# A fused attention and expert kernel on one Trainium2 core: the norms' work divided anew between VectorE and GpSimd, the finish of a batch at other steps, scatters at other places

## The chip, the cores and the metric

The kernel runs on 1 core of one Trainium2 chip. Its time is device microseconds of one launch, and of each version the median of several runs is given. Engines are TensorE (PE), VectorE (DVE), ScalarE (ACT), GpSimd (POOL) and SyncE (SP). Each runs its own instruction list in order, and semaphores tie the lists together.

## The reference

Input is `x`, 8 batches of 512 rows by 256 numbers, f16.

```
x = x + layernorm(attention(layernorm(x)))      # 16 heads of 16, causal, biases, f16
x = x + layernorm(ffn(layernorm(x)))            # 8 experts, 256 -> 688 -> 256, float32

layernorm(x) = (x - mean) / sqrt(var + 1e-5)    # along the 256
ffn: logits = x @ Ws + bs; the two best experts of each row, their logits through a softmax;
     out = sum over the two of weight * ((silu(x @ Wg[e]) * (x @ Wu[e])) @ Wd[e])
```

There are three norms per batch before the expert part's output: of the input (attention's own input), of the attention's output, and of the sum of the two (the experts' input). A fourth, of the experts' output, is done at the end in another way and isn't touched.

## The kernel before

**Groups and steps.** The attention part is 8 batches b of 4 groups g (four heads each), and a group is 12 steps. At each step TensorE computes one bank of transposed scores of this group (L1774), one bank of plain scores of the group two ahead (L1777), and from step 8 on products with the values (L1784). ScalarE turns each bank of transposed scores into exponentials in `pT` (L983). VectorE takes the row maxima of the plain scores (L1149, and L1162 from group 18 on), which TensorE needs two steps later. GpSimd sets to zero what lies above the diagonal: three cuts (L759) per group, released by steps 3, 7 and 11 of the exponentials. TensorE's values at step 8 wait for cut 0, those at step 10 for cut 1, those at step 2 of the next group for cut 2. A place in the lists below is a pair (group of the batch, step) or, for GpSimd, (group, cut).

**Everything else is woven in by hand-written lists** of such pairs: `EARLY_AT` and `TILE_AT` (TensorE's projections and transposes, before and from group 18 on), `AT_NEXT_NORM` (the input norm of batch b+1), `AT_FINISH` (12 parts that finish batch b-1: bias of the attention's output, statistics in two halves, moments, scaling in two halves, adding x, then again statistics, moments, and scaling into `rows`, the experts' input `xn2`), `AT_PLAN` (from batch 3 on, four parts that plan which expert the next tiles belong to), `AT_ROUTE` and `AT_SLOTS` (the choice of experts and of the row's place, in group 3), and `AT_SCATTER` (GpSimd's indirect DMAs of the routed rows to DRAM, 8 per batch in 4 pairs, from batch 2 on).

**From group 18 on** the first expert tiles (256 rows each) run beside the attention: TensorE's products (L1724, L1742), ScalarE's tanh and copies (L943, L955), VectorE's gate and product (L1338, L1346), and on GpSimd after each cut a subtraction (`tile_low`, L775), after cut 0 the scatter of the tile before (`store_tile`, two indirect DMAs, L785), and after cut 1 the taking over of the next tile's row numbers (`take_tile`, L768, L769). SyncE loads a tile once its plan is there and enough scatters have landed (L556 to L566). After group 31 the remaining tiles run alone to about 840 us, and then comes the last norm.

**A norm** is made in four stages. VectorE: statistics (`norm_stats`, L1115) and moments `mv` (`norm_moments`, L1122). GpSimd: `rsqrt` (L692 to L700), which adds epsilon to the variance, copies the mean, takes the power 0.5 and then the power -1. VectorE: `norm_scale` (L1125 to L1132), with mean and `rstd` as scalars per row. TensorE: transposes. `rsqrt` stands at three places in GpSimd's list: for the input norm ahead of cut (0, 0); for the norm of the attention's output after cut (1, 1) and the tile's work there; for the experts' input norm after cut (2, 0) and the tile's work there, so ahead of cut (2, 1). TensorE transposes the experts' input at step 11 of group 2 (`xn2T`), and ScalarE copies it out.

`hold` (L74) is a wait on a semaphore and one increment behind it, used where an instruction reads what its own engine has just written.

## Time and profile before

| | |
|---|---|
| median of 3 runs | 889.12 us (882.86 to 891.24) |
| profiled execution | 878.99 us, of which 877.2 us are its span |
| TensorE's clock granted, mean | 0.917 of full |
| TensorE, VectorE, ScalarE, GpSimd busy | 713.8, 615.1, 550.6, 444.1 us |
| woven part (attention and first 14 tiles) | to about 594 us |
| tiles alone, last norm | about 594 to 840 us, 840 to 877 us |

Times in rows are microseconds from the start of the span unless marked ns. "Idle before <- releaser" is how long an engine had stood before an instruction and whose signal came last. The clock granted is given in parts of 2.4 GHz: 1.00 is 2.4, 0.50 is 1.2 GHz. To separate the groups, the stretches of the tables run from ScalarE's eviction of the shifted queries in one group (L896, once per group, at step 7 or 8) to that in the next: 119.66, 131.08 and 148.83 us are those of groups 1, 2 and 3 of batch 1; 354.05, 373.41, 396.47 and 419.14 those of batch 5.

### The profile page before, as it was taken

The numbers are of one execution on the slowest core, as the hardware profiler recorded it, in microseconds if no ns is written. First come the engines' busy times: TensorE is split into PE (matmuls) and PEld (weight loads), VectorE is DVE, ScalarE is ACT, GpSimd is POOL, SyncE is SP. The second block draws the span as 40 slices with busy tenths as digits, with TensorE's granted clock in tenths as the row PEclk, the third lists the DMA queues.
The fourth block names the chain that finished last, engine by engine and source line by source line (L and its number), as shares of the span: only waits on it lengthen the run. The fifth ranks groups of instructions, "written<-read, shape, count | busy, mean of one in ns | idle before, by whom it ended". The sixth has DMA issues, their size and how long they took to land.

```text
span 877.2 us, 21718 instructions
## 1 busy us (share of the span) xinstructions
PE 713.8 (81%) x6822; PEld 470.2 (54%) x6822; DVE 615.1 (70%) x1960; ACT 550.6 (63%) x1122; POOL 444.1 (51%) x552
## 2 busy tenths in 40 slices
PE   3677677768777989988997899898979999999920
PEld 1244444444443355544554455466857888888810
DVE  5777898888877878897889778755744445444445
ACT  4588885857765667756676576565545555555536
POOL 3554433553624435664577457747564343343427
PEclk9689998998986599999999899999999999999965
DMA  6434231463251111221122021213345233232257
GB/s 194 139 118 147 91 115 44 147 191 108 94 174 49 35 31 21 44 55 20 20 43 52 11 32 38 53 23 56 50 99 145 44 43 45 44 46 42 38 138 268
DMA packets 74008, 69.09 MB, mean 79 GB/s; under 512 B 6832, under 2 KB 67888, under 8 KB 73904
## 3 DMA queue, kind: packets, MB, share of 16 engines
q1 hardware_dynamic: 60624, 53.23, 19.7%
q0 software_dynamic: 13280, 14.49, 11.6%
q8 instruction: 63, 1.03, 0.5%
q14 instruction: 41, 0.34, 0.1%
HBM read 34.04 MB, written 31.29 MB: 74 GB/s over the span
## 4 chain that ended last, share of the span: by engine, by line
PE 46%; DVE 31%; issue 8%; ACT 7%; POOL 5%; DMA 2%; SPq 0%; DVEq 0%; POOLq 0%; ACTq 0%
PE bank L1880 13%; PE bank L1902 10%; PE bank L1724 6%; DVE nmax L1149 5%; DVE unused L1162 5%; PE bank L1631 4%; PE bank L1742 3%; DVE stats L1115 3%; DVE stage L1338 2%; POOL gu_part L862 2%; DVE rows L1130 2%; PE bank L1662 2%; DVE gu_part L1364 2%; PE bank L1591 2%; PE bank L1618 1%
## 5 line engine op out<-in xcount | busy, mean ns | idle before, releaser
L983 ACT ACTIVATE pT<-bank 128x512 f16<-128x512 f32 (+1 forms) x384 | 200.0, 534 | 97.3 <-PE bank L1631 95.0
L759 POOL TENSOR_SCALAR_AFFINE_SELECT pT<-pT 128x512 f16<-128x512 f16 x128 | 87.9, 731 | 146.2 <-ACT pT L983 145.9
L1149 DVE TENSOR_REDUCE nmax<-bank 128x1 f16<-128x384 f32 (+2 forms) x216 | 126.2, 597 | 35.6 <-PE bank L1620 33.6
L1880 PE MATMUL bank<-tile_xT,gu_part 128*128 128x256 f16 (+1 forms) x1100 | 132.4, 275 | 6.9 <-DVE stage L1450 3.6
L1880 PEld LDWEIGHTS bank<-tile_xT,gu_part 128*128 (+1 forms) x1100 | 106.5, 100 | 29.9 <-issue 8.4
L1162 DVE CUSTOM_DVE_ANT_0 unused<-bank,mask 128x384 f16<-128x384 f32 (+2 forms) x224 | 103.5, 483 | 16.5 <-PE bank L1609 15.1
L1450 DVE SCALAR_TENSOR_TENSOR stage<-bank,stage 128x512 f32<-128x512 f32 (+1 forms) x100 | 55.5, 555 | 80.4 <-ACT stage L1036 70.4
L785 POOL DMA_INDIRECT expert_rows<-tile_y,tile_dest x52 | 83.4, 1603 | 55.0 <-ACT tile_y L968 46.4
L1902 PE MATMUL bank<-wd_part,stage 128*128 (+2 forms) x850 | 105.3, 277 | 2.5 <-ACT stage L1045 1.7
L1724 PE MATMUL bank<-tile_xT,gu_part 128*128 128x256 f16 (+1 forms) x616 | 90.2, 286 | 12.8 <-DVE stage L1346 12.3
L1902 PEld LDWEIGHTS bank<-wd_part,stage 128*128 128x128 f16 (+2 forms) x850 | 78.2, 99 | 23.4 <-issue 13.8
L1045 ACT ACTIVATE stage<-stage 128x512 f16<-128x512 f32 (+1 forms) x100 | 52.3, 523 | 57.8 <-DVE stage L1450 53.2
L1457 DVE TENSOR_TENSOR stage<-stage 128x512 f16<-128x512 f32 (+1 forms) x100 | 55.8, 558 | 37.3 <-ACT stage L1045 34.4
L1662 PEld LDWEIGHTS bank<-va,pT 128*128 128x128 f16 x1280 | 54.5, 98 | 46.9 <-issue 26.9
L1662 PE MATMUL bank<-va,pT 128*128 128x17 f16 x1280 | 67.5, 173 | 12.7 <-POOL pT L759 12.7
L145 POOL DMA_INDIRECT dispatch_rows<-rows,slot x64 | 66.8, 1043 | 19.7 <-issue 16.8
L1724 PEld LDWEIGHTS bank<-tile_xT,gu_part 128*128 (+1 forms) x616 | 58.1, 103 | 29.8 <-issue 18.7
L1631 PE MATMUL bank<-qT,kT 32*128 32x512 f16 (+3 forms) x256 | 72.7, 325 | 0.6 <-issue 0.3
L1742 PE MATMUL bank<-wd_part,stage 128*128 (+2 forms) x476 | 69.9, 281 | 0.0
L1609 PE MATMUL bank<-kT,qT 32*128 32x384 f16 (+2 forms) x224 | 64.3, 329 | 3.3 <-DVE nmax L1162 2.9
L943 ACT ACTIVATE stage<-bank 128x256 f32<-128x256 f32 x84 | 32.2, 383 | 50.4 <-PE bank L1724 46.3
L1036 ACT ACTIVATE stage<-bank 128x512 f32<-128x512 f32 (+1 forms) x100 | 45.2, 478 | 28.1 <-PE bank L1880 28.0
(201 smaller groups left out, 1433.2 us busy)
## 6 DMA issues: line engine op xcount, KB each, us to landing
expert_rows<-tile_in SPq DMA_DIRECT2D x8, 1024.0 KB
stage<-wg SPq DMA_DIRECT2D x8, 688.0 KB, 4.0
stage<-wu SPq DMA_DIRECT2D x8, 688.0 KB, 4.2
stage<-wd SPq DMA_DIRECT2D x8, 640.0 KB, 4.2
tile_in<-dispatch_rows SPq DMA_DIRECT2D x39, 130.0 KB
gu_part<-expert_rows SPq DMA_DIRECT2D x16, 256.0 KB, 6.1
out<-gu_part SPq DMA_DIRECT2D x16, 256.0 KB, 2.4
x_sb<-x SPq DMA_DIRECT2D x8, 256.0 KB
```

The lines of the kernel that those rows point to most:

```text
L145: gp.indirect_dma_start(out=xs_dram[:, :], in_=keep["rows"][:, t, r, :], in_offset=None, out_offset=bass.IndirectOffsetOnAxis(ap=keep["slo ...
L759: last = gp.affine_select(out=diagonal, in_=diagonal, compare_op=ALU.is_ge, fill=0.0, base=0, pattern=[[0, J], [1, P]], channel_multiplier=-1)
L785: gp.indirect_dma_start(out=ys_dram[:, :], in_=y_of(n)[:, t, :], in_offset=None, out_offset=bass.IndirectOffsetOnAxis(ap=dest[n % 2][:, t: ...
L983: sc.activation(pT[:, lo:hi], ST_BANK[i % 2][:, 0:hi - lo], ACT.Exp, scale=1.0 / INV_SCALE).then_inc(p_ready, 1)
L1149: v.tensor_reduce(columns, S_BANK[i % 2][:, 0:n * len(heads)].rearrange("p (j n) -> p j n", n=n), AX.X, ALU.max, negate=True).then_inc(s_m ...
L1162: last = v.tensor_tensor_reduce(out=unused[:, i % 2, at:at + n], in0=S_BANK[i % 2][:, at:at + n], in1=mask[:, T - n:T], scale=-1.0, scalar ...
L1631: last = mm(ST_BANK[i % 2][:, at:at + n], keys[rows, P * kt:P * (kt + 1)], qT[rows, g, P * kt:T], start=True, stop=True)
L1662: last = mm(OUT[:, qt, j, 0:HD + 1], pT[:, at:at + P], va[:, g, kt, j, :], start=(i == 0 and qt == 0), stop=(i == NF - 1 and qt == QT - 1))
L1724: last = mm(target, keep["gu"][part][:, bass.ds(col + (k * GU + at), width_)], tile_xT[n % 2][:, k, :], start=(s == 0), stop=(s == 2 * KD ...
L1742: last = mm(Y_BANK[:, D * t:D * (t + 1)], h[0:rows, c // 2, at:at + P], keep["wd"][w][0:rows, bass.ds(col + c * D, D)], start=(c == 0 and ...
L1880: last = mm(target, keep["gu"][part][:, bass.ds(col + (kd * GU + at), width_)], tile_xT[(WOVEN + m) % 2][:, kd, :], start=(s == 0), stop=( ...
L1902: last = mm(Y_BANK[:, D * t:D * (t + 1)], h[0:rows, c // 2, at:at + P], keep["wd"][w][0:rows, bass.ds(col + c * D, D)], start=(c == 0 and ...
```

## The change

Three things. **The norms:** VectorE now adds epsilon and copies the mean, directly behind the moments, and takes the reciprocal ahead of the scaling; GpSimd keeps one instruction, the power 0.5. Two holds come with it. **The steps:** `AT_FINISH` has its scaling of y at (1, 10) and (1, 11) instead of (2, 1) and (2, 2), and everything behind it one or two steps sooner, the last scaling at (2, 7) and (2, 8) instead of (2, 9) and (2, 10); `xn2T` goes from step 11 to 10; `AT_PLAN` goes from group 1 to group 0, steps 8 to 11. **GpSimd's order:** `rsqrt` for the two norms of the finish goes ahead of cut (1, 1) and ahead of cut (2, 0). The four pairs of scatters stood after cuts (0, 1), (0, 2), (1, 0) and (1, 2); now they stand at the beginning of group 0, after cut (0, 1), and at the beginnings of groups 1 and 2.

```diff
-        power = sb(stack, "power", [P, 2, QT], F32)
+        power = sb(stack, "power", [P, QT], F32)
...
-                    {"q": (1, 2), "k": (3, 4), "v": (5,), "max": (6, 7), "xn2T": (11,)},
+                    {"q": (1, 2), "k": (3, 4), "v": (5,), "max": (6, 7), "xn2T": (10,)},
...
-                   {"q": (1,), "k": (3,), "v": (5,), "max": (7,), "xn2T": (11,)},
+                   {"q": (1,), "k": (3,), "v": (5,), "max": (7,), "xn2T": (10,)},
...
-            return grp * NF + {"q": 3, "k": 5, "v": 7, "max": 8, "attT": 9, "xnT": 11, "y0": 1, "y1": 3, "xn2T": 12}[what]
+            return grp * NF + {"q": 3, "k": 5, "v": 7, "max": 8, "attT": 9, "xnT": 11, "y0": 1, "y1": 3, "xn2T": 11}[what]
...
-        AT_FINISH = ((1, 4), (1, 5), (1, 6), (1, 7), (2, 1), (2, 2), (2, 3), (2, 4), (2, 5), (2, 6), (2, 9), (2, 10))
-        AT_PLAN = ((1, 8), (1, 9), (1, 10), (1, 11))
+        AT_FINISH = ((1, 4), (1, 5), (1, 6), (1, 7), (1, 10), (1, 11), (2, 1), (2, 2), (2, 3), (2, 4), (2, 7), (2, 8))
+        AT_PLAN = ((0, 8), (0, 9), (0, 10), (0, 11))
...
-        AT_SCATTER = ((0, 1), (0, 2), (1, 0), (1, 2))
+        AT_SCATTER = ((0, None), (0, 1), (1, None), (2, None))
...
                def rsqrt(n):
...
-                    pool.wait_ge(var_ready, n + 1)
-                    gp.tensor_scalar(veps[:, :], mv[:, :, 1], LN_EPS16, None, ALU.add).then_inc(veps_ready, 1)
-                    gp.tensor_copy(mean[:, :], mv[:, :, 0]).then_inc(mean_ready, 1)
                     pool.wait_ge(veps_ready, n + 1)
-                    gp.tensor_tensor(std[:, :], veps[:, :], power[:, 0, :], ALU.pow).then_inc(std_ready, 1)
-                    pool.wait_ge(std_ready, n + 1)
-                    gp.tensor_tensor(rstd[:, :], std[:, :], power[:, 1, :], ALU.pow).then_inc(rstd_ready, 1)
+                    gp.tensor_tensor(std[:, :], veps[:, :], power[:, :], ALU.pow).then_inc(std_ready, 1)
...
-                ch.link(gp.memset(power[:, 0, :], 0.5))
-                ch.link(gp.memset(power[:, 1, :], -1.0))
+                ch.link(gp.memset(power[:, :], 0.5))
...
                def batch(b):
...
                     for g in range(G):
+                        if scattering and g == 0:
+                            pool.wait_ge(slot_ready, b - 1)
+                            pool.wait_ge(copy_ready, b - 1)
+                        if scattering and (g, None) in AT_SCATTER:
+                            scatter_rows(gp, keep, xs_dram, AT_SCATTER.index((g, None)), len(AT_SCATTER))
                         for c in range(CUTS):
                             at = (g, c)
                             if at == (0, 0) and not in_last:
                                 rsqrt(1 if first else 3 * b - 1)
+                            if at == (1, 1) and not first:
+                                rsqrt(3 * b - (1 if in_last else 0))
+                            if at == (2, 0) and not first:
+                                rsqrt(3 * b + 1 - (1 if in_last else 0))
                             cut(G * b + g, c)
...
                                 take_tile(n + 1)
-                            if at == (1, 1) and not first:
-                                rsqrt(3 * b - (1 if in_last else 0))
-                            if at == (2, 0) and not first:
-                                rsqrt(3 * b + 1 - (1 if in_last else 0))
...
                def norm_moments(n):
...
                     last.then_inc(var_ready, 1)
+                    hold(dve, var_ready, n + 1, spare)
+                    v.tensor_scalar(veps[:, :], mv[:, :, 1], LN_EPS16, None, ALU.add).then_inc(veps_ready, 1)
+                    v.tensor_copy(mean[:, :], mv[:, :, 0]).then_inc(mean_ready, 1)
...
                def norm_scale(dst, src, n, half):
                     if half == 0:
+                        dve.wait_ge(std_ready, n + 1)
+                        v.reciprocal(rstd[:, :], std[:, :]).then_inc(rstd_ready, 1)
                         dve.wait_ge(mean_ready, n + 1)
-                        dve.wait_ge(rstd_ready, n + 1)
+                        hold(dve, rstd_ready, n + 1, spare)
```

## Rows read from the trace of the kernel before

**Rows 1.** The page, busy time, share of the span and instructions of each engine

```profile
PE 713.8 (81%) x6822; PEld 470.2 (54%) x6822; DVE 615.1 (70%) x1960; ACT 550.6 (63%) x1122; POOL 444.1 (51%) x552
```

**Rows 2.** Windows: length, busy PE, PEld, DVE, ACT, POOL, then clock, DMA share, GB/s

```profile
119.66:131.08 11.42, 8.96 (x101) 5.46 (x101) 10.95 (x31) 9.06 (x19) 3.80 (x7) 1.00 0.44 129
131.08:148.83 17.75, 13.94 (x161) 8.77 (x162) 14.09 (x49) 10.71 (x21) 5.25 (x9) 0.81 0.16 49
354.05:373.41 19.36, 18.77 (x191) 11.68 (x188) 15.35 (x53) 14.61 (x33) 13.45 (x16) 1.00 0.27 51
373.41:396.47 23.06, 19.36 (x181) 11.03 (x179) 21.37 (x82) 13.85 (x32) 15.97 (x20) 0.93 0.26 56
396.47:419.14 22.67, 19.72 (x201) 11.61 (x198) 17.35 (x71) 14.31 (x33) 10.75 (x16) 0.92 0.09 15
504.76:523.08 18.32, 17.28 (x193) 10.57 (x191) 14.81 (x63) 13.05 (x32) 8.77 (x11) 1.00 0.15 23
```

**Rows 3.** Waits: who waited for whom, us in total, times, longest

```profile
POOL veps L695 <- DVE mv L1122: 53.4, 15, 5.9
...
PE bank L1662 <- POOL pT L759: 12.7, 10, 2.2
...
PE bank L1582 <- DVE rows L1130: 6.3, 6, 1.7
```

**Rows 4.** Timeline of TensorE: start, us, instruction, idle before it and releaser

```profile
135.37 0.38 PE L1662 MATMUL bank<-va,pT 128*128 128x17 f16 x8 [1.42 <-POOL pT L759]
...
462.79 0.36 PE L1662 MATMUL bank<-va,pT 128*128 128x17 f16 x8 [1.00 <-POOL pT L759]
...
488.26 0.62 PE L1582 MATMUL bank<-ident,rows 128*128 128x128 f16 x8 [1.66 <-DVE rows L1130]
...
566.48 0.36 PE L1662 MATMUL bank<-va,pT 128*128 128x17 f16 x8 [2.04 <-POOL pT L759]
```

**Rows 5.** Windows at half clock, the first, the longest and the last of six

```profile
135.40:141.50 6.10, 5.29 (x60) 3.42 (x61) 3.50 (x10) 2.39 (x4) 0.64 (x1) 0.50 0.38 118
...
247.80:254.70 6.90, 5.71 (x67) 3.88 (x68) 3.52 (x8) 2.76 (x5) 1.77 (x3) 0.51 0.91 302
...
568.80:571.60 2.80, 2.80 (x17) 1.45 (x16) 0.00 (x0) 1.72 (x3) 0.55 (x1) 0.50 0.18 48
```

**Rows 6.** Two lines of `rsqrt`: ns min/median/max, first and last start us

```profile
L698 POOL TENSOR_TENSOR std<-veps,power x24: 1040/1044/1077, 6.9 to 617.7; 128x4 f16<-128x4 f16 x24
...
L700 POOL TENSOR_TENSOR rstd<-std,power x24: 1007/1012/1072, 8.1 to 618.8; 128x4 f32<-128x4 f16 x24
```

**Rows 7.** Timeline, TensorE's first projection

```profile
13.35 1.01 PE L1591 MATMUL bank<-xnT,wq_sb 128*128 128x512 f16 x2 [1.89 <-POOL va L737]
```

**Rows 8.** Timeline of group 1 of batch 1, three engines

```profile
118.55 1.23 POOL L759 TENSOR_SCALAR_AFFINE_SELECT pT<-pT 128x512 f16<-128x512 f16 x2 [2.64 <-ACT pT L983]
...
120.92 0.37 DVE L1122 BATCH_NORM_AGGREGATE mv<-stats 128x2 f16<-128x6 f32 x4
...
122.16 0.35 PE L1662 MATMUL bank<-va,pT 128*128 128x17 f16 x8
```

**Rows 9.** Small VectorE instructions: one line's durations in ns, and two of the timeline

```profile
L1264 DVE RECIPROCAL wts<-den x8: 170/171/173, 152.8 to 644.1; 128x4 f32<-128x4 f32 x8
...
459.31 0.16 DVE L1306 TENSOR_TENSOR stock<-fill,next 128x8 f32<-128x8 f32 x1
459.62 0.19 DVE L1307 TENSOR_TENSOR whole<-stock,iota_t 128x32 f32<-128x32 f32 x1
```

**Rows 10.** The plan's scan: durations in ns, and one of the timeline

```profile
L1311 DVE TENSOR_TENSOR_SCAN cum_early<-one_early,new_tiles x6: 163/520/2348, 234.4 to 590.2; 128x8 f32<-128x8 f32 x6
...
461.69 2.20 DVE L1311 TENSOR_TENSOR_SCAN cum_early<-one_early,new_tiles 128x8 f32<-128x8 f32 x1
```

**Rows 11.** VectorE's scalings by shape: busy us, mean ns, idle before

```profile
L1130 DVE TENSOR_SCALAR rows<-y,mean,rstd 128x256 f16<-128x256 f16 x32 | 16.7, 622 | 1.8 <-POOL rstd L700 1.7
L1130 DVE TENSOR_SCALAR y<-y,mean,rstd 128x256 f16<-128x256 f16 x32 | 9.5, 345 | 0.1
```

More of the change, by code:

```diff
@@ L812, in batch @@
                             if at in AT_SCATTER and scattering:
-                                if at == AT_SCATTER[0]:
-                                    pool.wait_ge(slot_ready, b - 1)
-                                    pool.wait_ge(copy_ready, b - 1)
                                 scatter_rows(gp, keep, xs_dram, AT_SCATTER.index(at), len(AT_SCATTER))
```

## The prediction

> **What bounds the kernel now.** I read the page first: TensorE 81% busy, VectorE 70% [rows 1]. An average says little here, so I cut the attention part at the eviction of the shifted queries, which ScalarE does once per group near step 8, and asked for the busy time between two of them. The stretch from group 1 to group 2 of a batch is VectorE's: 10.95 of 11.42 us in batch 1, 21.37 of 23.06 us in batch 5. The next one, from group 2 to group 3, is nobody's: 17.75 us with VectorE at 14.09 and TensorE at 13.94; 22.67 us with 17.35 and 19.72 in batch 5. The stretch from group 0 to 1 of batch 5 is TensorE's, 18.77 of 19.36 us, with VectorE 4.0 us short of full; so is the one after group 3 of batch 6, which takes only 18.32 us [rows 2]. What makes the group 2 stretch long stands in the waits: TensorE waited 12.7 us for the causal cut, 6.3 us for the normalised rows that `xn2T` transposes, while GpSimd itself stood 53.4 us before the norms for VectorE's moments [rows 3]. Of the 12.7 us, 3.3 are three waits in group 1 of batches 5 to 7 (462.79 is one) and 0.9 is one in group 3; the other six stand in group 2, the first of 1.42 us at 135.37, the last of 2.04 at 566.48, 8.5 in all, and the longest wait for the rows is 1.66 us [rows 4]. Around them TensorE falls to half clock, 1.2 GHz instead of 2.4, in six stretches of 2.8 to 6.9 us, 31.6 us together, each begun in such a wait or at most 2.3 us behind one [rows 5].
>
> **The mechanism.** VectorE has the second norm's moments at step 6 of group 2; GpSimd then runs four instructions, two of them a power of 1.04 and 1.01 us [rows 6], and has the second cut of group 2 queued behind them; VectorE scales only at steps 9 and 10, and the transposes stand at step 11.
>
> **Sum, part by part.** All against the profiled execution: 877.2 us of span, 878.99 us as timed.
> - Start. The first norm's four GpSimd instructions and those behind them decide when TensorE projects at 13.35 us: it waits for GpSimd's last constant [rows 7]. One power of 1.01 goes, two small instructions move to VectorE and are paid there at about 0.3: **-0.8** (0 to -1.2).
> - Group 2's two waits. Moments come two steps sooner, GpSimd has one power (1.04) where it had about 2.4 us, the cut follows it with a whole step or more to spare, and the rows are scaled at steps 7 and 8 for transposes at step 10, so that there are two maxima between the last scale and the transposes as before, less one. Both waits sum to 14.8 us, the half clock costs at most half of 31.6, 15.8 us. Neither can be had in full, as VectorE's work comes next: group 2's stretch leaves it 3.7 us (batch 1) and 5.3 us (batch 5), stretches without such waits leave it 0.5 to 3.5 [rows 2]. That is 3.2 and 1.8 us to be had, 2.5 on average, in six batches: **-15** (-5 to -24).
> - Group 1's cut in batches 5 to 7. Two scatters stood between the store of a tile and the cut of step 8; now the pair comes a cut earlier and one power (1.04) stands there instead of 2.6 us. TensorE's three waits there, 3.3 us with the one of 1.00 shown [rows 4], mostly go: **-3** (0 to -3.3).
> - Group 1's cut in batches 1 to 4: a **new wait**. The root is now issued ahead of the cut, and waits for moments that VectorE delivers only after its step 7. In batch 1 they end at 120.92+0.37=121.29; VectorE's addition and the hand-over take some 0.35, the power 1.04, the two selects 1.23, with 0.1 between them: cut at 124.0. TensorE wants it at 122.16; before, the selects ran from 118.55 [rows 8]. So 1.9 us of new wait, 3 x 1.9 + 1.6 (batch 4) = 7.3 us. VectorE is full there and has the scaling of y to do in the meantime, which hides a third: **+5** (0 to +16, if each also costs a drop of the clock of 3 us as in group 2).
> - VectorE's new work. Per norm an addition, a copy and a reciprocal, and two holds. The reciprocal of this shape takes 171 ns and two small dependent instructions start 0.31 us apart (459.31, 459.62) [rows 9]: hold and addition 0.30, copy 0.08, reciprocal with its hold 0.31, together 0.69 us; 24 norms are 16.6 us. About half fall in stretches where VectorE is full: **+8** (+2 to +16.6).
> - The plan moves from group 1, steps 8 to 11, to group 0. It is 5.8 us of VectorE in a tile batch, and 2.2 of it is one scan that takes 163 ns elsewhere [rows 10]. Group 0 can hide 4.0 us less the 0.5 to 1.5 it needs anyway, so it grows by 2.4; group 1's stretch falls from 23.06 towards TensorE's 19.36, 3.5 us. Batches 5 and 6 win 1.1 each, batch 7 loses 1 since its group 1 is shorter: **-1** (-6 to +6). The tile loads that wait for the plan see it a group sooner, but also need the last pair of scatters, which stays where group 1 ends; nothing comes of it.
> - Scatters. The same eight per batch. The first pair now stands before the root of group 0, where GpSimd idles up to 5.9 us for moments [rows 3], and needs slots that VectorE has ready then: 0. If the slots were late, the cut of step 4 would slip, with 4 steps of cover. SyncE's loads of pieces and tiles are not behind anything new.
> - GpSimd's lighter load (1.4 us less per norm, 33 us): VectorE's scaling of the rows averages 622 ns against 345 for y [rows 11], which I put down to this, that GpSimd's cut runs beside it. At steps 7 and 8 GpSimd stores tiles instead: 32 x 0.28 = 9 us, mostly in full stretches of four batches: **-2** (0 to -5).
>
> Sum -0.8 -15 -3 +5 +8 -1 -2 = -8.8 us: 870.2 us on the profiled execution's own scale. That execution lies 10.1 us under the median of the runs, 889.12; on the median's scale I say **880 us**.
>
> A row against the change is the scan: 163 ns at best, 2348 ns at worst, and 2.20 us at 461.69 [rows 10], while GpSimd ran a select and a subtraction. The Trainium skill (SBUF — State Buffer, section Who interferes with whom) says that a VectorE instruction in a two-port mode, or with two inputs in SBUF, and a GpSimd instruction shut each other out for the whole instruction, and counts copies and scalar additions among those that can be. The scan agrees. By that rule the addition and the copy that come to VectorE can each be held like the scan, which is a rival below.
>
> **Rivals.**
> 1. *The clock holds.* For it: every long half-clock stretch of groups 2 comes with a wait that goes; group 0 to 1, full and unbroken, stays at 1.00 [rows 2]. Then waits and clock give -20, group 1 costs +2, the new work +6, the scaling -4 and the rest the same: -21, 868 us. Against it: VectorE is next, with 0.5 to 1.7 us to spare in group 1.
> 2. *The wait only moves.* The new wait of 1.9 us at step 10 of group 1 is as long as those in group 2 after which the clock fell. Three drops of 3 us more and only 12 for group 2: 12 us less gained, +3, 892; with the y-scaling hiding most of that wait, 888. I take **888 us**, no change.
> 3. *Slower: VectorE carries all of it.* Place: the stretches that lead up to group 2, where VectorE is full already. The 16.6 us all lie on the path (+8.6), small instructions being held by selects and subtractions as the scan was where they would still have found a gap; group 2's waits give only 8 because VectorE fills the gap (+7), and nothing hides the new wait (+2.3): 880+18 = **898 us**. It decides from about 17 us of VectorE time on the path: there the sum's gains of 22 less the 5 of the new wait are used up. The page named above would have it so, for additions and copies in tile batches. Against it: VectorE's small instructions of today mostly keep 160 ns, the scan aside.
> That the change does nothing at all would need TensorE not to wait for these two, and it does [rows 4]; so it is no case of its own but part of rival 2.
>
> **Numbers.** Forecast (880) 0.40, rival 1 (868) 0.24, rival 2 (888) 0.21, rival 3 (898) 0.15. A measurement of this kernel tells about 1%, 8.9 us, from no change: under 880.2 is faster, over 898 slower. Faster: half of the forecast's chance, all of rival 1, a tenth of rival 2: 0.20+0.24+0.02 = 0.46. Slower: half of rival 3 and the far ends of the others, 0.12. The rest, 0.42, is no change. The range runs from a little under rival 1 to just short of rival 3: 864 to 897; the forecast's own is 872 to 888.
>
> **What would show it.** Right: `xn2T` and the cut of group 2 no longer among TensorE's waits, stretches from group 2 to 3 of 15 and 20 us instead of 17.8 and 22.7, half clock there gone; group 1's waits down to nothing in batches 5 to 7, a wait of 1 to 2 us for the cut at its step 10 in batches 1 to 4; VectorE some 15 us busier less what the scaling gives back. Wrong: half clock now in group 1; small additions or copies of over 1 us on VectorE; group 0 of batches 5 and 6 longer by over 4 us; GpSimd waiting for slots at the start of a batch while TensorE waits for a cut.

## Result and the profile after

Side by side, the kernel before took 884.66 us (median of 6 runs) and the changed one **873.46 us** (864.54 to 877.49, 6 runs): a ratio of 0.9863 with a 95% interval of [0.9823, 0.9902]. A second measurement of both (`changed_again`, below) gave 0.9892 [0.9843, 0.9940]. The forecast was 880 against 889.12, a ratio of 0.990. The direction was right and the size nearly so.

The page after, the lines that answer to [rows 1]:

```profile
span 873.5 us, 21754 instructions
...
PE 709.9 (81%) x6822; PEld 470.0 (54%) x6822; DVE 623.2 (71%) x2032; ACT 550.9 (63%) x1122; POOL 411.5 (47%) x479
```

VectorE is 8.1 us busier, GpSimd 32.6 us less busy. The profiled execution took 875.25 us, only 3.7 less than that of before. The medians differ by 11.2. The profiled execution of before lies 5.7 us under the median of its runs, and that of after 1.8 us over its own. So the profiled pair can show where time moved, but not all of it.

TensorE's and GpSimd's waits after, to be read against [rows 3]: who waited for whom, us in total, times, the longest.

```profile
POOL std L695 <- DVE veps L1121: 80.6, 19, 7.1
...
PE bank L1663 <- POOL pT L753: 8.8, 11, 1.5
...
PE bank L1583 <- DVE rows L1131: 1.6, 2, 0.8
```

The wait for the normalised rows fell from 6.3 to 1.6 us, that for the cut only from 12.7 to 8.8. Of these 8.8, 4.6 are four new waits in group 1 of batches 1 to 4 (1.22, 1.06, 1.27, 1.05).

The windows after, for the five stretches of [rows 2] from batch 1, groups 1 and 2, and batch 5, groups 0, 1 and 2, and then two half-clock stretches in group 1 of batches 2 and 3. Columns: length, busy PE, PEld, DVE, ACT, POOL, granted clock, DMA share, GB/s.

```profile
121.27:135.03 13.76, 9.51 (x104) 5.55 (x105) 12.72 (x42) 9.07 (x20) 4.58 (x7) 1.00 0.36 109
135.03:151.01 15.98, 11.93 (x153) 7.64 (x153) 13.18 (x44) 10.64 (x21) 3.20 (x5) 0.89 0.18 52
358.78:381.56 22.78, 20.01 (x191) 12.19 (x188) 19.72 (x68) 15.21 (x33) 13.55 (x15) 0.93 0.21 42
381.56:401.77 20.21, 17.71 (x181) 10.39 (x179) 17.59 (x72) 13.88 (x33) 12.23 (x15) 1.00 0.27 55
401.77:420.94 19.17, 18.17 (x201) 11.13 (x198) 16.29 (x72) 14.07 (x32) 10.29 (x13) 1.00 0.17 23
181.50:189.00 7.50, 6.11 (x46) 3.33 (x47) 6.14 (x16) 2.75 (x6) 4.60 (x6) 0.54 0.33 115
240.00:247.00 7.00, 5.90 (x44) 3.32 (x45) 5.41 (x15) 2.85 (x6) 3.71 (x5) 0.52 0.19 55
```

Group 2's stretches shrank, 17.75 to 15.98 and 22.67 to 19.17 us, the second at full clock. Group 1's in batch 1 grew by 2.3. All stretches of the attention part, cut at the same evictions and summed over batches, in us:

| stretch from group | batches | before | after | difference |
|---|---|---|---|---|
| 0 | 1 to 4 | 54.8 | 57.9 | +3.1 |
| 1 | 1 to 4 | 56.8 | 63.4 | +6.6 |
| 2 | 1 to 4 | 72.2 | 63.5 | -8.7 |
| 0 (the plan's new place) | 5 to 7 | 57.9 | 65.5 | +7.6 |
| 1 | 5 to 7 | 65.4 | 57.4 | -8.0 |
| 2 | 5 and 6 | 46.4 | 38.2 | -8.1 |
| 3 | 1 to 6 | 101.1 | 103.7 | +2.6 |

That is -4.9; batch 0 and the start give +1.6 back, so the last of these evictions comes 3.3 us sooner. In the profile of `changed_again` the first six rows agree with these within 0.5 us, the last is 1.6 us longer, and the last eviction comes at 557.5 us (561.4 before, 558.1 here).

Groups 1 and 2 of batches 1 to 4 have to be read together, since VectorE's work moved across the line between them: with the finish two steps sooner, the second norm's moments and a row maximum now come before the eviction. In batch 1 VectorE is busy 12.72 us in group 1's stretch where it was 10.95, and 13.18 in group 2's where it was 14.09. Together the two rows give -2.1 us, and with group 0 batches 1 to 4 win nothing in this execution; the gain lies in batches 5 and 6.

From the last eviction to TensorE's last product it is 277.1 us in this execution, 277.6 before and 271.6 in the profile of `changed_again`, which has the same code. Differences of this size between executions are as large as the gain in the attention part, and with one profile of the kernel before, the traces don't show where its median is slower.

The timeline after, batch 1, group 1, to be read against [rows 8]: start, us, engine, instruction, idle before it and whose signal ended it.

```profile
122.53 0.37 DVE L1118 BATCH_NORM_AGGREGATE mv<-stats 128x2 f16<-128x6 f32 x4
...
123.05 0.17 DVE L1121 TENSOR_SCALAR veps<-mv 128x4 f16<-128x4 f16 x1
...
123.30 1.01 POOL L695 TENSOR_TENSOR std<-veps,power 128x4 f16<-128x4 f16 x1 [5.78 <-DVE veps L1121]
...
124.28 1.23 POOL L753 TENSOR_SCALAR_AFFINE_SELECT pT<-pT 128x512 f16<-128x512 f16 x2
...
125.56 0.36 PE L1663 MATMUL bank<-va,pT 128*128 128x17 f16 x8 [1.22 <-POOL pT L753]
```

This is the new wait as forecast: GpSimd stands 5.78 us for the addition, with the cut queued behind it, and TensorE then stands for the cut.

### The profile page after: what moved, and what is told of

Same layout as the page of the kernel before. It is cut to its first block, busy times and chain, and to the rows that moved or that the text cites. A ratio compares the mean times of both kernels' runs of the same rounds, so it can differ in the third digit from the quotient of the medians.

```text
span 873.5 us, 21754 instructions
## 1 busy us (share of the span) xinstructions
PE 709.9 (81%) x6822; PEld 470.0 (54%) x6822; DVE 623.2 (71%) x2032; ACT 550.9 (63%) x1122; POOL 411.5 (47%) x479
## 3 DMA queue, kind: packets, MB, share of 16 engines
q8 instruction: 63, 1.03, 0.5%
## 4 chain that ended last, share of the span: by engine, by line
PE 39%; DVE 12%; POOL 8%; issue 7%; ACT 3%; DMA 1%; another core or an unknown queue 1%; SPq 0%; DVEq 0%; POOLq 0%; ACTq 0%
PE bank L1881 13%; PE bank L1903 10%; PE bank L1725 5%; PE bank L1743 3%; DVE unused L1163 2%; POOL expert_rows L779 2%; PE bank L1632 2%; POOL gu_part L858 2%; POOL pT L753 2%; PE bank L1663 1%; DVE stage L1339 1%; DVE stage L1347 1%; POOL stage L769 1%; POOL std L695 1%; DVE whole L1308 1%
## 5 line engine op out<-in xcount | busy, mean ns | idle before, releaser
L753 POOL TENSOR_SCALAR_AFFINE_SELECT pT<-pT 128x512 f16<-128x512 f16 x128 | 90.8, 776 | 141.0 <-ACT pT L979 140.7
L145 POOL DMA_INDIRECT dispatch_rows<-rows,slot x64 | 65.4, 1023 | 28.9 <-issue 15.2
L1632 PE MATMUL bank<-qT,kT 32*128 32x512 f16 (+3 forms) x256 | 72.2, 323 | 0.4
L695 POOL TENSOR_TENSOR std<-veps,power 128x4 f16<-128x4 f16 x24 | 26.2, 1093 | 80.7 <-DVE veps L1121 80.6
```

What stands on the lines that cost most here:

```text
L145: gp.indirect_dma_start(out=xs_dram[:, :], in_=keep["rows"][:, t, r, :], in_offset=None, out_offset=bass.IndirectOffsetOnAxis(ap=keep["slo ...
L753: last = gp.affine_select(out=diagonal, in_=diagonal, compare_op=ALU.is_ge, fill=0.0, base=0, pattern=[[0, J], [1, P]], channel_multiplier=-1)
L1632: last = mm(ST_BANK[i % 2][:, at:at + n], keys[rows, P * kt:P * (kt + 1)], qT[rows, g, P * kt:T], start=True, stop=True)
```

## Experiments

The ratios are to the kernel before, measured side by side with the version in question, with 95% intervals. "Root" is the instruction at L695 of the changed kernel. Stretches and waits are those of one profiled execution of each version.

**1. The norms alone** (`norm_only`): GpSimd's order, all steps and the scatters as before.

```diff
-        AT_FINISH = ((1, 4), (1, 5), (1, 6), (1, 7), (1, 10), (1, 11), (2, 1), (2, 2), (2, 3), (2, 4), (2, 7), (2, 8))
-        AT_PLAN = ((0, 8), (0, 9), (0, 10), (0, 11))
+        AT_FINISH = ((1, 4), (1, 5), (1, 6), (1, 7), (2, 1), (2, 2), (2, 3), (2, 4), (2, 5), (2, 6), (2, 9), (2, 10))
+        AT_PLAN = ((1, 8), (1, 9), (1, 10), (1, 11))
# also: xn2T at step 11, both finish roots behind cut and tile work, AT_SCATTER = ((0, 1), (0, 2), (1, 0), (1, 2))
```

> Only the norms' work is divided anew; steps, the root's places in GpSimd's list and the scatters are as before. My theory, that what the change brought is the shorter way from moments to cut and rows in group 2: GpSimd has one power there where it had 2.4 us, so the waits for the second cut of group 2 (8.5 us in six) lose about 1.4 us each, and VectorE pays 0.69 us per norm, half of it on the path (8 us): ratio 0.995 to 1.003 of before. Rival, that VectorE's 16.6 us all lie on the path: ratio 1.006 to 1.012. Rival, that a lighter GpSimd is the whole of the gain: ratio 0.986.

Measured: 891.73 us, 1.0064 [1.0029, 1.0100]. That is over the range of my theory and in that of the first rival, VectorE's 16.6 us all on the path. Group 2's waits for the cut went but for 0.68 and 1.03 us; the stretches of batches 1 and 2 lasted 17.74 and 17.72 us (17.75 and 17.58 before). So GpSimd's time saved by itself bought nothing there: the next wait in line, for the rows, stood at 0.95 to 1.66 us in all seven batches.

**2. Everything but the norms** (`all_but_norms`): GpSimd keeps four instructions, all else as changed.

```diff
-                    pool.wait_ge(veps_ready, n + 1)
-                    gp.tensor_tensor(std[:, :], veps[:, :], power[:, :], ALU.pow).then_inc(std_ready, 1)
+                    pool.wait_ge(var_ready, n + 1)
+                    gp.tensor_scalar(veps[:, :], mv[:, :, 1], LN_EPS16, None, ALU.add).then_inc(veps_ready, 1)
+                    gp.tensor_copy(mean[:, :], mv[:, :, 0]).then_inc(mean_ready, 1)
+                    pool.wait_ge(veps_ready, n + 1)
+                    gp.tensor_tensor(std[:, :], veps[:, :], power[:, 0, :], ALU.pow).then_inc(std_ready, 1)
+                    pool.wait_ge(std_ready, n + 1)
+                    gp.tensor_tensor(rstd[:, :], std[:, :], power[:, 1, :], ALU.pow).then_inc(rstd_ready, 1)
```

> The changed kernel with GpSimd's four instructions per norm back and VectorE's three gone: earlier finish, plan in group 0, root ahead of the cuts, scatters as changed. My theory: the gain is one of places, but four instructions (2.4 us) ahead of cut (1, 1) make the new wait there 1.4 us longer in seven batches (some +7 us) and VectorE is 8 us lighter: ratio 0.983 to 0.990, the changed kernel's own 0.986 within noise. Rival, that the norms are what makes the places possible: ratio 0.993 or more, with a wait of over 2.5 us for the cut at step 10 of group 1 in batches 1 to 3 and half clock behind each.

Measured: 896.11 us, 1.0156 [1.0122, 1.0189]; my expectation failed, the rival's held. The waits (who, whom, total, times, longest):

```profile
PE bank L1664 <- POOL pT L759: 27.5, 15, 2.8
...
PE bank L1584 <- DVE rows L1132: 1.3, 3, 0.8
```

With two powers ahead of the cut, TensorE stands 1.8 to 2.8 us at it in every group 1 and 1.4 to 1.8 in most groups 2. The norms that cost 0.6% alone are worth 2.6 to 2.9% (1.0156 against 0.9892 and 0.9863, not all measured side by side) once the root stands ahead of the cut.

**3. Everything but the scatters** (`all_but_scatters`): they stay at their old places.

```diff
-        AT_SCATTER = ((0, None), (0, 1), (1, None), (2, None))
+        AT_SCATTER = ((0, 1), (0, 2), (1, 0), (1, 2))
```

> The changed kernel with the scatters where they were, after cuts (0, 1), (0, 2), (1, 0) and (1, 2). My theory: the pair after cut (1, 0) puts 2.6 us between the store and the root with cut (1, 1) behind it in batches 4 to 7, so TensorE's wait for that cut in batches 5 to 7 is 2 to 3 us instead of 0.4: 5 to 8 us lost in all, ratio 0.992 to 0.996. Rival, that scatters cost nothing where they stood: ratio 0.986 as in the changed kernel.

Measured: 886.05 us, 1.0036 [1.0004, 1.0067], a bigger loss than either range had. GpSimd's timeline in group 1 of batch 5 (columns as above):

```profile
376.43 1.57 POOL L779 DMA_INDIRECT expert_rows<-tile_y,tile_dest  x1 [0.30 <-issue]
378.31 0.99 POOL L145 DMA_INDIRECT dispatch_rows<-rows,slot  x1 [0.30 <-issue]
379.60 0.97 POOL L145 DMA_INDIRECT dispatch_rows<-rows,slot  x1 [0.30 <-issue]
380.59 1.07 POOL L695 TENSOR_TENSOR std<-veps,power 128x4 f16<-128x4 f16 x1
381.63 1.23 POOL L753 TENSOR_SCALAR_AFFINE_SELECT pT<-pT 128x512 f16<-128x512 f16 x2
```

and TensorE's wait at its end, then the windows of this stretch and of the half clock behind the same wait in batches 5, 6 and 7:

```profile
382.91 0.36 PE L1661 MATMUL bank<-va,pT 128*128 128x17 f16 x8 [2.99 <-POOL pT L753]
```

```profile
376.14:400.29 24.15, 19.10 (x181) 11.05 (x179) 19.33 (x72) 13.88 (x32) 13.97 (x17) 0.93 0.24 51
384.00:387.50 3.50, 3.50 (x32) 2.11 (x31) 3.03 (x12) 1.37 (x4) 2.79 (x6) 0.52 0.02 7
466.00:473.00 7.00, 6.52 (x50) 3.68 (x50) 4.72 (x12) 1.84 (x5) 5.23 (x8) 0.51 0.04 13
548.00:555.00 7.00, 5.41 (x37) 3.06 (x37) 4.54 (x9) 1.60 (x4) 5.83 (x10) 0.51 0.04 12
```

Two scatters (1.3 us each with the gap) and the root stand in one row ahead of the cut, TensorE waits 2.99, 2.98 and 2.90 us for it in the three batches (0.43, 0.39 and 0.38 in the changed kernel), and a half-clock stretch begins in or up to 1.2 us behind each. VectorE stands 1.03, 1.02 and 0.59 us for the same root. The stretches of group 1 are 3.9, 5.2 and 4.4 us longer than in the changed kernel, 13.5 us together, as much as the loss of 13 to 15 us by the ratios. But the last eviction comes only 6.6 us later (564.7 for 558.1): group 0 of batches 5 to 7 is 4.4 us shorter here and batch 0's first stretch 2.2. So this one profile shows half of the loss.

**4. Everything but the plan** (`all_but_plan`).

```diff
-        AT_PLAN = ((0, 8), (0, 9), (0, 10), (0, 11))
+        AT_PLAN = ((1, 8), (1, 9), (1, 10), (1, 11))
```

> The changed kernel with the plan in group 1, steps 8 to 11, beside the scaling of y. My theory: group 0's stretch falls from 22.8 and 20.6 us to some 19.5 in batches 5 and 6, group 1's rises from 20.2 to 24, because VectorE has no room there: 1 to 5 us lost over five batches, ratio 0.987 to 0.992. Rival, that it is as good in either place: 0.986. Rival, that group 0 was the wrong place (its stretch grew by 3.4 us in batch 5 and 3.1 in batch 7): 0.982 or less.

Measured: 876.12 us, 0.9911 [0.9877, 0.9944]. The interval overlaps both of the changed kernel, so the times don't settle what the plan's move is worth. The stretches do show what it did: those of group 1 in batches 5 to 7 last 24.24, 23.87, 24.07 us here (20.21, 20.25, 16.90 changed), those of group 0 18.92, 18.43, 18.96 (22.78, 20.60, 22.15). In batches 5 to 7 the move wins 14.8 and costs 9.2, net 5.6 us. It costs in batches 3 and 4 too, where there is a plan as well: group 0 takes 12.11 and 17.35 us here, 13.13 and 18.83 with the plan in it. That is 2.5 of the 3.1 us that group 0 of batches 1 to 4 grew.

**5. The scatters alone** (`scatters_only`), and **6. norms and scatters** (`norms_and_scatters`), both with all steps and roots as before.

```diff
-        AT_SCATTER = ((0, 1), (0, 2), (1, 0), (1, 2))
+        AT_SCATTER = ((0, None), (0, 1), (1, None), (2, None))
# 6 also: the three places of the norms as changed
```

> The kernel before with the scatters alone where the change has them. Taken out of the changed kernel they cost 1.7% (1.0036 against 0.9863). Theory 1, that the pair after cut (1, 0) matters because the root now stands ahead of cut (1, 1) behind it: alone they save only the three waits for that cut of batches 5 to 7, 3.3 us in the trace of before: ratio 0.995 to 0.999. Theory 2, that the scatters cost 1.7% wherever the norms stand: ratio 0.983 to 0.988.

> The kernel before with the norms' new division and the scatters' new places; finish, plan, xn2T and the root's places as before. Norms alone gave 1.0064, with 1.5 to 2.0 us of wait for cut (1, 1) in batches 5 to 7 and the waits for the rows at step 11 of group 2 still 1.0 to 1.7 us in all seven batches. Theory 1, that group 2 is long because the rows come at step 10 for a transpose at 11, whatever the norm costs: the scatters take only group 1's waits away, ratio 0.997 to 1.003, group 2's stretches stay at 17.7 us in batches 1 and 2 and at 22 or more in batches 5 and 6. Theory 2, that lighter norms and scatters are the gain and the steps are incidental: ratio 0.986 to 0.990, group 2's stretches short.

Measured: 877.89 us, 1.0000 [0.9970, 1.0030], and 886.45 us, 1.0093 [1.0066, 1.0121]. In 5 the three waits of group 1 for the cut are gone, as forecast, and nothing is won: these stretches last 24.16, 24.22 and 22.58 us, 1.1, 1.2 and 3.3 more than before, while those of group 0 of the same batches are 4.1 us shorter together. A small instruction of the plan (L1308) takes 2.99 and 2.98 us in batches 5 and 6, beside two selects and a subtraction of GpSimd. What else lengthens them wasn't tried. In 6, the window of group 2 in batch 1 and the waits:

```profile
131.54:149.35 17.81, 13.55 (x161) 8.75 (x162) 14.04 (x52) 10.72 (x22) 3.97 (x6) 0.81 0.16 48
```

```profile
PE bank L1583 <- DVE rows L1131: 9.0, 7, 1.7
...
PE bank L1663 <- POOL pT L753: 3.3, 4, 1.1
```

The wait for the cut fell from 12.7 to 3.3 us, that for the rows rose from 6.3 to 9.0, and the stretch is as long and at the same clock as in [rows 2]. In this theory 1 was right and theory 2 wrong, but the time lies over both ranges. Group 1's stretches of batches 5 to 7 are 8.7 us longer than before; in two of them VectorE's new copy takes 3.04 and 3.02 us (see 12). So two of the three parts together lose 0.9%; the places in `AT_FINISH`, the root ahead of the cut and the plan turn this into a gain.

**7. The root behind the cut where the new wait stood** (`root_behind_early`): in batches 1 to 4 the root of (1, 1) goes behind the cut.

```diff
-                            if at == (1, 1) and not first:
+                            if at == (1, 1) and b > 4:
                                 rsqrt(3 * b - (1 if in_last else 0))
...
                             cut(G * b + g, c)
+                            if at == (1, 1) and 0 < b <= 4:
+                                rsqrt(3 * b)
```

> The changed kernel with the root of group 1 behind cut (1, 1) in batches 1 to 4 and ahead of it, as changed, in batches 5 to 7. My theory, that the new waits for this cut (1.22, 1.06, 1.27 and 1.05 us) and the half clock they bring (6.8 us in batches 2 and 3) are a cost the change could do without: the waits go, group 1's stretches of batches 1 to 3 fall from 13.8, 15.0 and 15.0 us by 1 to 2 us each, ratio to before 0.979 to 0.984. Rival, that VectorE carries those stretches and the wait is hidden: no change, 0.986, with the waits gone all the same.

Measured: 864.16 us, 0.9827 [0.9802, 0.9853], with number 8 **the fastest version**, though the interval still touches those of the changed kernel. The windows of group 1 in batches 1, 2 and 3, then TensorE's waits (this kernel's lines stand two higher):

```profile
121.30:134.50 13.20, 9.69 (x104) 5.49 (x105) 12.62 (x42) 9.06 (x20) 3.50 (x6) 1.00 0.37 114
178.86:192.18 13.32, 10.72 (x104) 6.12 (x104) 12.74 (x42) 9.17 (x18) 5.55 (x8) 0.87 0.60 192
235.23:248.43 13.20, 9.69 (x104) 5.48 (x104) 12.62 (x42) 7.85 (x17) 6.11 (x9) 1.00 0.43 137
```

```profile
PE bank L1665 <- POOL pT L753: 3.2, 5, 1.5
```

The four waits are gone and the half clock at 240 with them. Of the half clock near 182, in batch 2, one half is still there (the mean clock of its stretch is 0.87), so the wait hadn't caused all of it. The stretches fall from 13.76, 15.02 and 14.97 us (batch 4: 19.70 to 18.36). They are now VectorE's, 12.6 to 12.7 us busy. The four stretches are 5.4 us shorter, batches 1 to 4 as a whole 4.0: that is what the new wait cost the changed kernel in its profile. Groups 1 and 2 of batches 1 to 4 now take 121.6 us together, where the kernel before had 129.0.

**8. The same with the plan split** (`root_early_plan_split`).

```diff
-        AT_PLAN = ((0, 8), (0, 9), (0, 10), (0, 11))
+        AT_PLAN = ((0, 9), (0, 11), (1, 8), (1, 9))
```

> The kernel of the run before this one with the plan at (0, 9), (0, 11), (1, 8) and (1, 9). If VectorE's load per stretch decides, halving the plan's 5.8 us between group 0 (which took 22.8 and 22.2 us with all of it in batches 5 and 7) and group 1 is better than either: 0.3 to 0.5% under the run before. If it is held instructions, single ones of 2 us where GpSimd's subtraction runs, it depends on chance places: within 0.3% either way. If group 1 has no room at all (24 us with the plan in it), it is 0.2 to 0.4% worse.

Measured: 863.37 us, 0.9842 [0.9814, 0.9869], the same as 7. The gain that "VectorE's load per stretch decides" asked for isn't there.

**9. The changed kernel again** (`changed_again`, without an edit) beside **10. VectorE's new instructions twice** (`vector_twice`).

```diff
+                    ch.link(v.tensor_scalar(again[:, 0, :], mv[:, :, 1], LN_EPS16, None, ALU.add))
+                    v.tensor_copy(again[:, 1, :], mv[:, :, 0])
...
+                        ch.link(v.reciprocal(again[:, 2, :], std[:, :]))
```

> The changed kernel once more, so that it stands on the same chip as the runs beside it: ratio to before 0.986 within 0.3%. If it comes at 0.983 or less, the kernel with the root behind the cut in batches 1 to 4 (0.9827 elsewhere) is no better than it.

> The changed kernel with VectorE's three small instructions of each norm done twice, into a scratch tile nobody reads: 0.6 to 0.7 us more of VectorE per norm, 15 us over 24 norms, and nothing else. My theory, that half of it lies on the path (the +8 us of my sum): ratio to the changed kernel 1.007 to 1.012. Rival, that VectorE carries the whole woven part: 1.015 or more. Rival, that it is hidden: 1.003 or less.

Measured: 866.83 us, 0.9892 [0.9843, 0.9940], and 881.95 us, 1.0069 [1.0038, 1.0099]. The changed kernel came 0.3% over the 0.986 expected, within its interval. The two medians, measured side by side, differ by 15.1 us, and with the spread of the runs the difference is some 12 to 20 us. Read off the trace, the added instructions and holds take 0.39 us behind the moments and 0.32 ahead of the scaling, 17.0 us over 24 norms. So nearly the whole length is paid, as the rival had it; "half of it" is refuted. The price doesn't come as plain length only. In the profile of 10, group 2 of batch 5, whole and its half-clock part:

```profile
406.60:431.44 24.84, 23.77 (x201) 13.07 (x198) 18.09 (x73) 14.55 (x33) 9.62 (x12) 0.73 0.12 18
412.00:425.50 13.50, 13.39 (x97) 7.03 (x95) 8.49 (x35) 6.82 (x13) 1.77 (x4) 0.50 0.04 11
```

This stretch is 5.7 us longer than in the changed kernel, at a mean clock of 0.73 instead of 1.00.

**11. The root of (2, 0) behind the cut** (`root20_behind`) and **12. the root of (1, 1) behind the cut in all batches** (`root11_behind`).

```diff
-                            if at == (2, 0) and not first:        # 12: (1, 1), and rsqrt(3 * b - ...)
-                                rsqrt(3 * b + 1 - (1 if in_last else 0))
                             cut(G * b + g, c)
...
+                            if at == (2, 0) and not first:
+                                rsqrt(3 * b + 1 - (1 if in_last else 0))
```

> The changed kernel with the root of the second norm behind cut (2, 0), the tile's subtraction and the store, where it was before. My theory: in batches 1 to 4 nothing changes (GpSimd idles there before the moments anyway); in batches 5 to 7 two indirect DMAs of 1.9 us stand ahead of the root, so VectorE waits for it at step 7 and the second cut comes a power later: 1 to 3 us in each, ratio to before 0.990 to 0.996. Rival, that the earlier steps alone are what counts: 0.986.

> The changed kernel with the root of the first norm behind cut (1, 1) in all batches, in batches 5 to 7 also behind the tile's subtraction and the taking over of the next tile (1.2 + 1.2 + 0.5 us). Batches 1 to 4 as in the better variant (0.9827). My theory: in batches 5 to 7 VectorE, which scales at step 10, stands 1 to 2 us for the root each time: ratio 0.985 to 0.990. Rival, that VectorE comes late enough at step 10: 0.981 to 0.984, so the root never had to go ahead of this cut.

Measured: 869.28 us, 0.9933 [0.9901, 0.9965], and 875.68 us, 0.9986 [0.9954, 1.0019].

Number 11 is in the range expected, and VectorE does stand 1.50, 0.81 and 2.17 us for the root in group 2 of batches 5 to 7. But beside it the changed kernel had 0.9892 [0.9843, 0.9940], which overlaps, so the loss isn't clear of noise.

Number 12 is over both ranges. In batches 1 to 3 it is number 7, and its stretches of group 1 agree within 0.01 us; in batch 4 the root stands behind the taking over of the first tile as well, and the stretch is 19.94 us for 18.36. The stretches of group 1 in batches 5 to 7 last 23.07, 23.12 and 20.84 us, where the changed kernel has 20.21, 20.25 and 16.90. VectorE's timeline in batch 5, then GpSimd's beside it, then what TensorE waits for:

```profile
377.30 0.43 DVE L1121 TENSOR_SCALAR veps<-mv 128x4 f16<-128x4 f16 x1
377.61 3.05 DVE L1122 CAST mean<-mv 128x4 f32<-128x4 f16 x1
380.57 0.68 DVE L1163 CUSTOM_DVE_ANT_0 unused<-bank,mask 128x512 f16<-128x512 f32 x1
```

```profile
377.71 1.80 POOL L753 TENSOR_SCALAR_AFFINE_SELECT pT<-pT 128x512 f16<-128x512 f16 x2
378.90 1.72 POOL L769 TENSOR_TENSOR stage<-stage 128x512 f16<-128x512 f32 x1
...
381.19 1.05 POOL L695 TENSOR_TENSOR std<-veps,power 128x4 f16<-128x4 f16 x1
```

```profile
381.31 0.39 PE L1610 MATMUL bank<-kT,qT 32*128 32x512 f16 x1 [1.25 <-DVE nmax L1163]
```

The copy of the means, 164 ns in the median, lasts 3.05 us, from 0.10 us before the selects until 0.04 us after the end of the subtraction. The row maximum behind it is late, TensorE stands 1.25 us and the clock falls (windows of this kernel, batches 5, 6, 7):

```profile
383.00:386.50 3.50, 3.50 (x32) 2.10 (x31) 3.30 (x12) 1.37 (x4) 2.48 (x3) 0.52 0.02 7
472.00:479.00 7.00, 6.79 (x37) 3.03 (x38) 5.72 (x22) 3.41 (x7) 0.25 (x1) 0.52 0.37 103
553.50:561.00 7.50, 7.50 (x40) 3.58 (x39) 4.67 (x14) 2.56 (x5) 0.98 (x1) 0.54 0.34 93
```

In batches 6 and 7 the copy takes 0.74 and 0.16 us, but the root comes so late behind the tile's work that VectorE stands 1.3 and 1.2 us before the reciprocal, and TensorE 1.71 and 2.00 us for the gate's product behind it. The copy was held in `norms_and_scatters` too, 3.04 and 3.02 us in batches 5 and 6. In the changed kernel it never lasts longer than 0.37 us. There GpSimd waits for the addition ahead of the cut, so addition and copy are over when the selects begin. With the root behind the cut it depends on how the two queues happen to stand: in `norm_only`, also with the root behind, no copy is longer than 0.35 us. So the root ahead of the cut costs a wait in the batches without tiles; in those with tiles it keeps the copy out of the selects' way and gives VectorE its root in time.

## Why the prediction was right, and where its terms were not

**Group 2's two waits, -15: right.** The wait for the rows went from 6.3 to 1.6 us and the three waits of group 2 for the cut in batches 1 to 3 are gone. Of the table's -8.7 us for batches 1 to 4 a part is VectorE's work that moved to group 1. Number 7, which has no new wait, gives the size better: groups 1 and 2 of batches 1 to 4 took 7.4 us less than before there, and group 2 of batches 5 and 6 gave 8.1 in the changed kernel. That is 15.5, with VectorE's new work already paid in it. Experiments 1, 2 and 6 show that this needed both the shorter root and the earlier steps. "Half clock there gone" holds for batch 5 but not for batch 1, where the clock is 0.89.

**Group 1's new wait, +5: right in place and price, not in length.** Four waits of 1.05 to 1.27 us instead of 1.9 and 1.6, since TensorE itself came later: counted from the eviction, it was ready after 3.07 us (125.56 less 1.22, less 121.27), where the working had it after 2.50 (122.16 less 119.66). Number 7 prices them at 4.0 to 5.4 us. "Half clock now in group 1" was named as a sign against the forecast; it came in batches 2 and 3, and was paid out of group 2's gain; half of that in batch 2 stayed without the wait too.

**VectorE's new work, +8: mis-sized.** Number 10 measured nearly the whole of such work on the path, 15.1 us for 17.0. The step that failed is "about half fall in stretches where VectorE is full". It counted full stretches of the kernel before. That VectorE was next in line in more of them once the waits on GpSimd were gone is my reading: number 10 prices a second set of these instructions on top of the change, and no run isolates the first set there. Rival 3 had this part right, and norms alone at +0.6% point the same way.

**Scatters, 0, and group 1's cut in batches 5 to 7, -3: mis-sized, since costed one at a time.** By themselves the scatters' places are worth 0 (-0.3% to +0.3%, number 5). With the root ahead of the cut they decide whether 1 or 3.6 us stand before it, and are worth 1.0036 against 0.9863 or 0.9892, 1.4 to 1.7%, 13 to 15 us (3). The term had the slots ready at the start of a batch; in fact GpSimd stands 1.2 to 3.3 us there for VectorE's rows (L1280) from batch 2 on. It cost nothing visible: group 0 of batches 1 to 4 takes 57.8 us with the scatters at their old places (3) and 57.9 with the new.

**The plan, -1: mis-sized.** It is -5.6 us by the stretches of batches 5 to 7; the times of number 4 don't settle it. Group 1 gave 14.8, 4.9 a batch where 3.5 was assumed; group 0 paid 9.2, 3.1 a batch where 2.4 was (the working's own numbers allow 2.3 to 3.3). The 2.5 us that it costs group 0 of batches 3 and 4 the sum didn't have. The move didn't free the plan of held instructions, it only changed which one is held: L1308, not the scan. VectorE's and GpSimd's timelines of the changed kernel in batch 5:

```profile
360.66 2.19 DVE L1308 TENSOR_TENSOR whole<-stock,iota_t 128x32 f32<-128x32 f32 x1
```

```profile
361.06 1.74 POOL L769 TENSOR_TENSOR stage<-stage 128x512 f16<-128x512 f32 x1
```

**GpSimd's lighter load, -2: smaller than its working.** The scaling of the rows gave 3.2 us of VectorE, 16.7 to 13.5 [rows 11], not the 9 that it would give at y's pace; y itself takes 1.0 more, and the input norm's scaling 0.8 more (11.8 to 12.6). The groups after: busy us, mean ns, idle before.

```profile
L1131 DVE TENSOR_SCALAR rows<-y,mean,rstd 128x256 f16<-128x256 f16 x32 | 13.5, 504 | 1.1
...
L1131 DVE TENSOR_SCALAR y<-y,mean,rstd 128x256 f16<-128x256 f16 x32 | 10.5, 372 | 1.1
```

**The start, -0.8: right for the projection.** TensorE's first projection comes at 12.62 instead of 13.35 [rows 7], and now waits for ScalarE:

```profile
12.62 1.01 PE L1592 MATMUL bank<-xnT,wq_sb 128*128 128x512 f16 x2 [1.27 <-ACT xnT L878]
```

What it is worth isn't settled: the first eviction of the table comes 0.6 us later than before in this execution (55.1 for 54.5 us) and 1.1 sooner in `changed_again` (53.4).

**Rival 3, held small instructions:** real in numbers 6 and 12, but in the changed kernel only for the plan's, not for the norms'. The Trainium skill (SBUF — State Buffer, section Who interferes with whom) says that a VectorE instruction in a two-port mode and a GpSimd instruction shut each other out for the whole instruction, copies among them. The copy of 3.05 us agrees: it ends 0.04 us after a subtraction that follows the selects without a gap, though by the trace's start times it began 0.10 us before the first of them.

The mis-sized terms offset one another: some 7 us more for VectorE against 5 more from the plan and 10 or more from the scatters. Put into the sum they would give about -17 us, where the two ratios give -10 to -12, so prices taken from leaving out one part at a time overlap and can't simply be added. On the scale of the profiled execution, for which it was worked out, the sum said -8.8 and the profiled pair shows -3.7. The mechanism of group 2 and the place of the new wait were foreseen; that the total was nearly met is in good part luck.

**Open.** A stretch of half clock of 37 to 55 us lies between 263 and 324 us in all versions, that of before included, with TensorE busy 32.3 of 37.5 us in it before the change; what starts it wasn't tried, and its length differs from trace to trace. The earlier steps were never run by themselves, without the roots' new places: their share is known only as what is left when the other parts alone don't win. What makes the part behind the attention differ by 6 us between executions isn't known.

## What to carry to other kernels

Parts of a change that act on one queue aren't additive: here the scatters and the norms were worth nothing and a loss by themselves (0 and +0.6%, together +0.9%), and the whole 1.1 to 1.4% less time; cost a queue at the point where all parts meet, with everything ahead of the late instruction in one row. When work is moved to an engine that is next in line, count its full length (here 15.1 of 17.0 us). A wait for another engine holds up everything queued behind it, so where it stands is to be chosen for each phase of the kernel: here ahead of the cut with tiles and behind it without, which gave the 0.9827 of number 7.

## What the runs showed of the hardware

- A small VectorE copy, 128x4, can last 3.05 us instead of 0.16. It ended 0.04 us after the last of two selects and a subtraction of GpSimd, and hadn't been let in between them (number 12; 3.04 and 3.02 in number 6).
- In number 3, where TensorE waited 2.99, 2.98 and 2.90 us and half clock followed, the stretches were 3.9, 5.2 and 4.4 us longer than in the changed kernel with waits of about 0.4. VectorE's waits for the same root are part of this.
- A GpSimd power of 128x4 takes 1.04 us; VectorE's reciprocal of the same shape takes 0.17, its addition 0.17 and copy 0.16.
